# An attention and ternary layer: swapped rotation pairs on neighbouring partitions, reciprocals spread by two transfers, and a new order of all work

## What is computed

```python
y = x * rsqrt(mean(x * x) + 1e-6) * rms_w            # (2, 1024, 512)
q, k, v = split(y @ w_in.T)                          # 32 query heads of 64, 8 key and 8 value heads
q, k = rope(q), rope(k)                              # pairs (i, i + 32) of a head are rotated:
#   concat([x1 * cos - x2 * sin, x2 * cos + x1 * sin])
attn = softmax(where(causal, q @ k.T / 8, -inf))     # each key head serves 4 query heads
x = layernorm(x + (x + (attn @ v) @ w_out.T))
x = layernorm(x + ternary(x) @ (ternary_w(weight) + rram).T)
```

## Time and profile before

| | |
|---|---|
| median of 3 runs | 1394.53 us (1389.77 to 1396.01) |
| profiled execution, its time | 1395.41 us |
| its span, first to last instruction | 1393.6 us |
| mean granted clock of PE | 0.984 of 2.4 GHz |
| busy: PE, DVE, ACT, POOL | 1260.4, 1128.3, 1028.9, 756.4 us |
| swap transfers | 320 issues, 64 KB each |
| spread transfers | 128 issues, 128 KB each |

### The profile page before, as it was taken

How to read it: one execution, slowest core, us unless ns; L and a number is a source line. 1 busy time by engine, 2 the same in 40 slices (tenths; PEclk the granted TensorE clock), 3 DMA queues, 4 the chain that set the end, 5 groups by cost and what they waited for, 6 DMA issues and landing times.

```text
span 1393.6 us, 29101 instructions
## 1 busy us (share of the span) xinstructions
PE 1260.4 (90%) x9632; PEld 810.3 (58%) x9632; DVE 1128.3 (81%) x2934; ACT 1028.9 (74%) x2199; POOL 756.4 (54%) x776
## 2 busy tenths in 40 slices
PE   4689899998999989998999989998999989998887
PEld 2356565665665656655666656655666656555565
DVE  4588777877897778978898778977888778888987
ACT  5678668777787768777787868867787777777765
POOL 1356554464545547365544646365554745598556
PEclk9799999999999999999999999999999999999999
DMA  6011111111111111111110111111011111121012
GB/s 206 25 31 52 40 33 33 46 39 43 35 48 35 45 31 38 48 33 49 31 51 25 43 35 43 49 30 51 24 38 49 35 40 44 43 65 32 13 40 94
DMA packets 45174, 62.06 MB, mean 45 GB/s; under 512 B 10464, under 2 KB 27104, under 8 KB 45024
## 3 DMA queue, kind: packets, MB, share of 16 engines
q1 hardware_dynamic: 45024, 60.20, 14.6%
HBM read 34.74 MB, written 4.46 MB: 28 GB/s over the span
## 4 chain that ended last, share of the span: by engine, by line
PE 50%; DMA 12%; DVE 10%; POOL 8%; SPq 7%; issue 7%; ACT 5%; DVEq 0%; POOLq 0%; ACTq 0%
PE x L1174 12%; PE t L1219 11%; PE s L1162 9%; PE ot L1127 8%; PE x L1202 7%; DMA spread<-recip_rows 5%; DVE prob L997 3%; DMA swapped<-flat 3%; SPq L594 3%; DMA recip_rows<-turned 3%; SPq L578 3%; DVE prob_lo L1090 2%; POOL flat L740 2%; POOL swapped L736 2%; POOL flat L738 2%
## 5 line engine op out<-in xcount | busy, mean ns | idle before, releaser
L1090 DVE SCALAR_TENSOR_TENSOR prob_lo<-t,prob_hi 128x512 f16<-128x512 f32 x576 | 393.0, 684 | 56.4 <-ACT prob_hi L793 54.4
L793 ACT ACTIVATE prob_hi<-t 128x512 f16<-128x512 f32 x576 | 338.9, 590 | 134.8 <-PE t L1219 130.3
L825 ACT ACTIVATE prob<-prob,neg_max 128x896 f32<-128x896 f32 (+7 forms) x512 | 392.3, 768 | 34.1 <-DVE neg_max L997 31.1
L1219 PE MATMUL t<-ident,prob 128*128 128x128 f32 x2304 | 358.5, 279 | 28.7 <-DVE prob_lo L1090 24.9
L1162 PE MATMUL s<-k_t,q_t 128*128 128x512 f16 (+3 forms) x1536 | 345.4, 328 | 38.9 <-DVE neg_max L997 23.8
L997 DVE CUSTOM_DVE_ANT_0 prob<-s,mask,neg_kappa 128x512 f32<-128x512 f32 (+3 forms) x512 | 320.4, 643 | 56.9 <-PE s L1162 44.5
L1219 PEld LDWEIGHTS t<-ident,prob 128*128 128x128 f32 x2304 | 266.2, 142 | 125.0 <-DVE prob_lo L1090 37.5
L766 POOL TENSOR_TENSOR o_lo<-o_raw,o_hi 128x256 f16<-128x256 f32 x128 | 86.3, 674 | 300.3 <-ACT o_hi L893 298.5
L1162 PEld LDWEIGHTS s<-k_t,q_t 128*128 128x128 f16 x1536 | 141.1, 98 | 122.9 <-DVE neg_max L997 38.8
L1127 PE MATMUL ot<-prob_hi,v_sb 128*64 128x256 f16 x2304 | 203.8, 277 | 0.0
L736 POOL TENSOR_TENSOR swapped<-swapped,sin_sb 128x512 f32<-128x512 f32 (+1 forms) x93 | 118.9, 1278 | 104.0 <-DMA swapped<-flat 102.6
(11 more groups left out here) (103 smaller groups left out, 1690.2 us busy)
## 6 DMA issues: line engine op xcount, KB each, us to landing
swapped<-flat SPq DMA_DIRECT2D x320, 64.0 KB, 2.0
spread<-recip_rows SPq DMA_DIRECT2D x128, 128.0 KB
recip_rows<-turned SPq DMA_DIRECT2D x512, 0.5 KB
raw<-L_attn_w_in SPq DMA_DIRECT2D x8, 768.0 KB, 4.7
raw<-L_attn_w_out SPq DMA_DIRECT2D x8, 512.0 KB, 3.7
out<-acc SPq DMA_DIRECT2D x16, 256.0 KB, 2.0
acc<-L_attn_x SPq DMA_DIRECT2D x3, 1024.0 KB, 10.3
acc<-L_attn_x SPq DMA_DIRECT2D x4, 256.0 KB, 3.8
```

The source lines that it names most:

```text
L793: act.activation(prob_hi[:, u % P_RING, :], t_ps[u % 2][:, :], ACT.Copy, scale=P_SCALE).then_inc(prob_hi_done, 1)
L825: act.activation(row, row, ACT.Exp, bias=neg_max[:, kk % 4, h:h + 1], scale=-1.0, accum_out=total[:, kk % 4, h:h + 1]).then_inc(ex_done, 1)
L1090: dve.scalar_tensor_tensor(out=prob_lo[:, u % P_RING, :], in0=t_ps[u % 2][:, :], scalar=P_SCALE, in1=prob_hi[:, u % P_RING, :], op0=ALU.mu ...
L1219: mm = pe.transpose(t_ps[u % 2][:, at:at + P], prob_row(s, h)[:, j * P:(j + 1) * P], ident[:, :])
```

## The change

Three things are changed; what is computed stays the same.

1. The host orders the rows of q and k in each head so that the two members of a rotation pair stand on neighbouring partitions, with the cos and sin tables to match. A swap then exchanges odd and even partitions: two transfers with a partition step of 2, of 64 rows for a query chunk and 32 for a key chunk, in place of four or two transfers of 32 rows.
2. A spread is two transfers of 64 rows, one per head pair, each with a source of 64 (step 0) by 256.
3. All tables of places are new. Of these the diff shows the lines for tiles (0, 6), (1, 2) and (1, 3) of the middle pass (places of the scores, of `ex`, then of `rc` and `rs`) and of its output lags (`on`, `oh`, `op`, counted from the last unit of the tile): in `OUTPUT` the 7th triple is tile (0, 5), whose `on` comes to place 204 before and 213 now, the 12th is tile (1, 2), place 340 before and 343 now.

```diff
 def swaps(n):
-    return sum(32 if m % 3 == 0 else 64 for m in range(n, -1, -2))
+    return 32 * len(range(n, -1, -2))
...
 MIDDLE = dict(
-     ((114, 120, 129, 133, 143, 146, 152, 155), (155, 144, 156, 156), 190, 201),
-     ((249, 260, 269, 272), (304, 300, 293, 307), 306, 323), ((284, 287, 301, 302), (311, 313, 321, 321), 327, 364),
+     ((110, 119, 129, 132, 144, 149, 153, 160), (156, 138, 160, 162), 189, 224),
+     ((246, 246, 262, 269), (280, 271, 274, 290), 302, 355), ((283, 288, 305, 309), (298, 304, 317, 324), 331, 374),
...
-    OUTPUT=((15, 14, 49), (31, 45, 63), (32, 54, 60), (73, 75, 97), (51, 68, 85), (41, 49, 94), (44, 75, 97),
-     (28, 45, 61), (19, 26, 36), (23, 41, 46), (28, 32, 55), (12, 46, 75), (28, 49, 60), (32, 37, 52), (23, 51, 87),
+    OUTPUT=((14, 26, 48), (39, 51, 60), (32, 50, 62), (54, 63, 100), (63, 66, 84), (64, 70, 114), (53, 66, 90),
+     (28, 41, 63), (15, 21, 41), (22, 32, 52), (32, 33, 55), (15, 55, 75), (38, 48, 64), (15, 59, 76), (17, 55, 87),
...
-                            wait(sp, spread_in[n], g, 16 * NT, 16 * (kk // 2))
+                            wait(sp, spread_in[n], g, 32 * NT, 32 * (kk // 2))
...
-                            rows = row_d[n].rearrange("(a c) q -> a (c q)", a=2).unsqueeze(1).to_broadcast([2, DH, 2 * P])
-                            sp.dma_start(spread[:, n, :, :].rearrange("p c q -> p (c q)"), rows
-                                         ).then_inc(spread_in[n], 16)
+                            for a in range(2):
+                                rows = row_d[n, 2 * a:2 * a + 2, :].rearrange("c q -> (c q)")
+                                sp.dma_start(spread[a * DH:(a + 1) * DH, n, :, :].rearrange("p c q -> p (c q)"),
+                                             rows.unsqueeze(0).to_broadcast([DH, 2 * P])).then_inc(spread_in[n], 16)
...
-                            for i in range(4 if e[3] < 2 else 2):
-                                sp.dma_start(swapped[i * 32:(i + 1) * 32, n % 2, :],
-                                             flat[(i ^ 1) * 32:((i ^ 1) + 1) * 32, n % 2, :]
+                            rows = P if e[3] < 2 else DH
+                            for i in range(2):
+                                sp.dma_start(swapped[i:rows:2, n % 2, :], flat[1 - i:rows:2, n % 2, :]
                                              ).then_inc(swapped_in[n % 2], 16)
...
-        "cos_dram": np.ascontiguousarray(np.tile(cos.T, (4, 1))),
+        "cos_dram": np.ascontiguousarray(np.tile(np.repeat(cos.T, 2, 0), (2, 1))),
...
+    q, k = (some.reshape(NG, -1, 2, DH // 2, width).swapaxes(2, 3).reshape(NG, -1, width) for some in (q, k))
```

More of the change, by code:

```diff
@@ L100 @@
 FIRST = (
[8 rows of a table removed]
[8 rows of a table added]
     ('ex', 2, 1, 3))
 OPENING = dict(
-    SCORES=(((0, 0, 7, 8), (16, 4, 12, 15), 35, 61), ((9, 23, 30, 39), (43, 34, 40, 42), 52, 116),
[11 rows of a table removed]
-    PROJECT=((((1, 4, 4, 11), (8, 4, 13, 30), (20, 8, 33, 43)), 10),
[4 rows of a table removed]
[L129 to L138, removed]
@@ L140 @@
-MIDDLE = dict(
-    SCORES=(((0, 0, 0, 3), (6, 1, 0, 4), 8, 55), ((3, 9, 14, 21), (21, 34, 28, 36), 91, 94),
[11 rows of a table removed]
-    PROJECT=((((52, 84, 72, 94), (110, 118, 132, 152), (161, 128, 185, 194)), 96),
[3 rows of a table removed]
[L157 to L161, removed]
-    OUTPUT=((15, 14, 49), (31, 45, 63), (32, 54, 60), (73, 75, 97), (51, 68, 85), (41, 49, 94), (44, 75, 97),
-     (28, 45, 61), (19, 26, 36), (23, 41, 46), (28, 32, 55), (12, 46, 75), (28, 49, 60), (32, 37, 52), (23, 51, 87),
-     (17, 37, 61), (23, 117, 110)))
@@ L166 @@
-FINAL = dict(
-    SCORES=(((2, 2, 3, 6), (15, 0, 13, 22), 27, 62), ((10, 13, 16, 23), (33, 29, 34, 33), 43, 75),
[10 rows of a table removed]
[L178 to L186, removed]
[5 rows of a table removed]
+    SCORES=(((0, 10, 11, 11), (3, 21, 15, 13), 25, 59), ((14, 18, 26, 28), (37, 21, 29, 32), 86, 108),
[11 rows of a table added]
@@ new lines @@
+    PROJECT=((((3, 0, 9, 14), (6, 17, 14, 25), (22, 22, 35, 45)), 13),
[4 rows of a table added]
+    SQUARES=(5, 9),
+    NORMS=((0, 11), (13, 19), (23, 23), (24, 26), (30, 40), (49, 61), (91, 143), (161, 174)),
+    NORM_O=(2, 15),
+    W_OUT=(39, 40),
+    LOAD=208,
+    NORM_W=(240, 277),
+    W_IN=(294, 301, 310, 316),
+    OUTPUT=((23, 101, 263), (17, 20, 49), (26, 39, 61), (47, 58, 74), (55, 73, 92), (46, 60, 71), (21, 64, 94),
+     (46, 51, 91), (15, 30, 40), (29, 37, 60), (59, 57, 85), (49, 63, 98), (47, 68, 117), (47, 100, 116),
+     (79, 76, 93), (27, 45, 61), (23, 124, -31)))
@@ new lines @@
+MIDDLE = dict(
+    SCORES=(((0, 0, 1, 8), (14, 0, 2, 12), 29, 71), ((10, 19, 20, 33), (35, 43, 37, 45), 89, 89),
[11 rows of a table added]
+    PROJECT=((((45, 43, 102, 133), (108, 129, 139, 166), (162, 169, 172, 194)), 97),
[3 rows of a table added]
+    NORM_O=(25, 34),
+    W_OUT=(42, 47),
+    LOAD=21,
+    NORM_W=(79, 109),
+    W_IN=(247, 263, 292, 292),
+    OUTPUT=((14, 26, 48), (39, 51, 60), (32, 50, 62), (54, 63, 100), (63, 66, 84), (64, 70, 114), (53, 66, 90),
+     (28, 41, 63), (15, 21, 41), (22, 32, 52), (32, 33, 55), (15, 55, 75), (38, 48, 64), (15, 59, 76), (17, 55, 87),
+     (17, 33, 60), (23, 117, 110)))
@@ new lines @@
+FINAL = dict(
+    SCORES=(((0, 1, 5, 5), (0, 4, 8, 9), 43, 71), ((11, 14, 18, 28), (18, 42, 28, 37), 57, 103),
[10 rows of a table added]
+    PROJECT=((((4, 34, 34, 81), (43, 35, 84, 147), (160, 169, 191, 198)), 139),
+     (((199, 210, 220, 256), (223, 251, 283, 307), (267, 281, 292, 317)), 243)),
+    NORM_O=(0, 11),
+    W_OUT=(30, 40),
+    FFN_IN=((31, 77), (92, 148), (160, 188), (236, 262)),
+    OUTPUT=((14, 13, 32), (16, 28, 60), (20, 53, 60), (36, 40, 69), (46, 57, 114), (36, 84, 134), (71, 105, 123),
+     (58, 75, 92), (19, 33, 50), (41, 48, 73), (58, 59, 82), (47, 61, 76), (62, 70, 91), (47, 64, 97), (45, 63, 104),
+     (39, 54, 67), (38, 25, 75)),
+    LAYER=((323, 346, 371, 379, 392, 396, 417), (342, 356, 386, 394, 406, 408, 498),
[5 rows of a table added]
@@ L1067, in events @@
                             wait(dve, pv_done, g, BODY, b * UNITS + first_unit(s + 1))
-                            wait(dve, spread_in[kk % 2], g, 16 * NT, 16 * (kk // 2 + 1))
+                            wait(dve, spread_in[kk % 2], g, 32 * NT, 32 * (kk // 2 + 1))
                             wait(dve, o_lo_done, g, 2 * NT, kk)
@@ L1245, in shape_constants @@
     return {
-        "cos_dram": np.ascontiguousarray(np.tile(cos.T, (4, 1))),
-        "sin_dram": np.ascontiguousarray(np.tile(np.concatenate([-sin.T, sin.T], 0), (2, 1))),
+        "cos_dram": np.ascontiguousarray(np.tile(np.repeat(cos.T, 2, 0), (2, 1))),
+        "sin_dram": np.ascontiguousarray(np.tile(np.stack([-sin.T, sin.T], 1).reshape(DH, seq), (2, 1))),
         "ident_dram": np.eye(P, dtype=f), "tri_dram": later,
```

## The result

The changed kernel takes 1302.23 us (median of 4 runs, 1301.82 to 1302.79), the kernel before 1394.55 us beside it: ratio 0.9344, 95% interval [0.9321, 0.9366]. That is 92 us less, where 42 were forecast; 1302 lies outside the range given. The direction was right, the size less than half of what came.

A forecast was written before the change was run, and what follows sets the result against it. PE was taken as the bound, with 10.7 us open per middle pass. Six passes at 5.0 us (30) plus 12.3 at the ends gave 42.3 us off 1395.4, so 1352 us; own range 1336 to 1366, 8 in 10 within 1328 to 1382.

The forecast's parts named there:

- the ends: Opening and final pass: swap 3.4 and 4 us in the opening, spread 1.9 and 3 in the final; 12.3 us saved.
- smaller gaps: PE's idle time in a middle pass outside the four largest gaps: 3.1 us, with no saving counted.
- place (3): Tile (1, 2), middle pass: spread behind (1, 3)'s row transfers; DVE idles 2.5 us, PE's 2.04 + 1.47 become 1.5.
- 0.7 for POOL: Loss per middle pass on POOL: a rope and an hl pair now ahead of o_lo of tile (0, 7).
- place (1): First query chunk's swap ahead of row transfers, o_lo before its rope: PE's 2.07 us gap goes, 0.4 left for POOL.
- The bound: PE, busy 149.32 of 160 us in a middle pass, bounds the kernel; at most 10.7 us per pass to gain.
- The spread's size: First spread issue to use takes 2.6 us; each spread that is waited for comes 1.9 us earlier.
- Rival 1: The gain is real but other waits eat half of it: 1373 us; chance 0.18 together with the no-gain split rival.
- the split brings nothing: Rival 2: two spread transfers gain nothing, second half lands 0.6 us later: 1375 us; chance 0.18 together with Rival 1.
- Rival 4: Slower: the interleaved swap lands late, at 5.8 us, and delays o_lo and the output product: 1417 us; chance 0.09.
- Rival 3: Nothing changes: waits move by the same amount elsewhere, POOL's ropes above all: 1392 us; chance 0.07.
- Places (1) and (2): Second is the spread behind PE's gap before 613.46: DVE has 6.7 us for 4.4, so the 2.03 us go.

The follow-up runs named there:

- e2: The changed kernel's new order with both transfers (spread and swap) of the kernel before: 1338.18 us.
- e3: The kernel before, old order, with only the spread split into two transfers: 1343.2 us.
- e1: The kernel before, old order, with both new transfers (spread and swap): 1325.02 us.
- e8: The kernel before with both new transfers and, on SyncE alone, no swap ahead of its own projection: 1317.84 us.
- e9: The changed kernel with its two spread transfers split by columns, each all 128 partitions from a source with outer dimension 2: 1354.97 us.
- mirrored kernel: The changed kernel with, on SyncE alone, five swaps of a middle pass put ahead of their projection again by the steps of before: 1378.98 us.

## Why the prediction was wrong

**What failed: the idle time that the sum left to PE in a middle pass, and the share taken for the ends.** The six middle passes were to give 30 us and the ends 12.3; they gave 62.7 and 31.3. For a middle pass 5.0 us were forecast and 10.4 measured (62.7 / 6). The sum left 5.7 us of idle time there: 3.1 of smaller gaps, 1.5 at place (3), 0.7 for POOL and 0.4 at place (1). 1.5 were left in all. PE's busy time, which the sum took as fixed, fell by another 2.0.

**Place (3).** It was to leave DVE 2.5 us idle and PE 1.5 at tile (1, 2). It was worked out for the wrong tiles: the two `o_raw` of the earlier trace rows belong to (1, 1) and (1, 2), not to (1, 2) and (1, 3). The place in the changed kernel, on DVE:

```profile
455.47 0.17 DVE L1009 RECIPROCAL recip<-total 128x4 f32<-128x4 f32 x1
...
456.87 0.41 DVE L998 CUSTOM_DVE_ANT_0 prob<-s,mask,low_max 128x128 f32<-128x128 f32 x1 [0.98 <-PE s L1163]
...
458.13 0.42 DVE L1071 SCALAR_TENSOR_TENSOR o_raw<-ot,spread 128x256 f32<-128x256 f32 x1
...
461.49 0.42 DVE L1071 SCALAR_TENSOR_TENSOR o_raw<-ot,spread 128x256 f32<-128x256 f32 x1
```

No idle time stands before either `o_raw`. The first row is the reciprocal of (1, 3), the last the `o_raw` of (1, 2): 6.0 us lie between them, 4.8 of work (the `o_raw` of (1, 1) among it) and 1.2 of waits for PE and ACT, where the forecast counted 1.9 of work and needed 4.4. Both waits of the earlier trace rows went, which gives back the 1.5. The place is tight all the same: in e2, the same order with the spread of before, DVE idles 2.1 us there in the median of the middle passes.

**The queue was not read.** The earlier trace rows show the rows of (1, 1) issued at 642.03, and the forecast took that time as given. DVE had turned them long before; on SyncE a swap and a load stand in between:

```profile
636.66 0.21 DVE L1012 STREAM_TRANSPOSE turned<-recip 128x32 f32<-128x32 f32 x1
```

```profile
640.09 1.21 SPq L594 DMA_DIRECT2D swapped<-flat  x2
641.34 0.58 SPq L548 DMA_DIRECT2D raw<-L_attn_w_out  x1
642.03 1.29 SPq L578 DMA_DIRECT2D recip_rows<-turned  x4
```

From 636.9 the rows were ready and stood behind that swap, for which SyncE waited until ACT's `flat` was made (639.47 to 640.07). Undoing such blocks alone is worth 26.4 us in the six middle passes (956.6 - 930.2), 4.4 in each; beside the new transfers 7.4 in the six (911.0 - 903.6).

**Small waits were taken to stay.** The forecast left 3.1 us of smaller gaps, 0.4 at place (1) and 0.7 of POOL's in each pass. The gaps that are shown shrank to 1.0 (0.78 and 0.25 above), and PE's loss from POOL at (0, 7) did not come. Which experiment takes away which of the smaller gaps was not followed.

**The bound.** "No faster engine can give more than 10.7 us" was nearly reached, 10.4: 8.4 of idle time and 2.0 of PE's busy time. The second was no term at all. Some of it is the clock, 1.00 in after's middle passes and 0.50 for some 3 us after a gap in before: three times 3.3 us at half the clock are 5 of the 12 us in six passes. The rest goes with the number of PE's gaps: before has 61 of over 0.15 us in the middle passes; e3, e1, e8 and after, none of which has a drop of the clock there, have 50, 36, 28 and 18, and PE is busy 891.1, 888.1, 886.7 and 884.7 us. Why a gap lengthens the busy time is open.

**The spread's size.** 0.55 + 2.0 = 2.6 us was forecast. A 64-row transfer lands 2.6 us after its issue, as the page has it, and there are two issues: 3.2 us from the first issue to `o_raw` where that is tightest, so 1.3 us less than before and not 1.9. At (0, 5) it was 2.0, since the spread of before took 5.3 there. The size was nearly right, and so was the number of spreads waited for in a middle pass, three. The number at the ends was not.

**The rivals.** Rival 1, that other waits eat half of the gain, fell: more came than was forecast. That the split brings nothing (1375 us) is refuted by e3, and that was the rule that the forecast weighed: the Trainium skill ("DMA: Bandwidth & Descriptors", Rules for kernel authors) advises against two transfers to disjoint halves of the partitions, as they serialize. Here they gain 51 us, since the one transfer instead of them ran on two engines. The same section's limit to as many engines as the outer dimension counts agrees with e9. Rival 4, the late swap, falls too: it decided from a landing of 4.9 us, and the slowest landing is 4.0. Tile `swapped` in after, issue ns and waits:

```profile
L596 SPq DMA_DIRECT2D swapped<-flat x192: 465/595/1372, 26.0 to 1184.4; - x192
...
  POOL swapped L737: 25.1, 20
...
DMA to landing us min/median/max: 1.9/2.1/4.0
```

POOL's waits for swaps fall from 102.6 to 25.1 us. Every second partition costs nothing in the median at the same size (2.0 us for 64 KB, before and after); a query transfer, now 128 KB, takes 2.1. Rival 3 had these waits moving elsewhere; they went.

**Places (1) and (2)** came as forecast: the gaps before 593.37 and 613.46 have no counterpart. PE's idle time by `o_lo` is 11.9 us in before and 2.8 in e2, that by `acc` before a projection 10.3 and none in e2, so the order alone does both; in e3 the shorter spread alone also does the second (0.4 left) and not the first (9.6).

**The ends.** Forecast 7.4 for the opening and 4.9 for the final pass; measured 15.3 and 16.0. They are passes with the same waits, and were priced by one swap, one spread and a share. DVE's idle time ahead of `o_raw` alone falls from 11.4 and 9.0 us there to 2.2 and 0.6. Of the 15.3 and 16.0 us, 13.3 and 10.9 come with the transfers alone.

## What to carry to other kernels

For a queue that works in order, list what it waits for and what ready work stands behind each wait; moving entries that stand too early behind their producer was worth 30 us here without any faster transfer, and the reverse cost 77. When the cure of a wait is priced, count the wait over the whole span by its consumer's row ("issue" included), not by the few largest gaps of the bound engine in one pass. Shorter transfers and earlier issues buy the same slack, so price each alone and both together.

## What was not expected of the hardware

A TensorE gap of some 2 us cost more than itself. In before the wait of 1.92 us was followed by some 3 us of the lower clock, as shown above; in the mirrored kernel, after PE had been idle for 4.79 us:

```profile
455.00:458.00 3.00, 0.00 (x0) 0.00 (x0) 0.49 (x2) 0.00 (x0) 0.00 (x0) 0.99 0.13 44
458.00:461.00 3.00, 2.48 (x20) 1.57 (x22) 2.96 (x9) 0.39 (x2) 0.00 (x0) 0.50 0.11 33
```

Over all middle passes of the mirrored kernel:

```profile
215.30:1185.40 970.10, 904.94 (x7035) 584.74 (x7034) 780.08 (x2090) 728.22 (x1573) 515.20 (x487) 0.98 0.12 39
```

In after PE is busy 884.7 us there, at a clock of 1.00. So 20 of the 76 us that the mirror costs there are longer work and not waiting. The mean clock is lower by 0.02, which over 970 us makes 19, part of it while PE was idle. Other gaps of 2 us, those of the earlier trace rows among them, were followed by a clock of 1.00. Why the one and not the other was not tried.
